# A decoder kernel: the norm's inverse deviation made by GpSimd instead of ScalarE in two of its attention stages

## The reference

```python
def _layernorm(x, axis=-1, eps=1e-05):
    m = jnp.mean(x, axis=axis, keepdims=True)
    v = jnp.var(x, axis=axis, keepdims=True)
    return (x - m) / jnp.sqrt(v + eps)
...
    x = _layernorm(x + _L0_attn_ref(x, ...), axis=-1)            # causal attention, softplus squared
    x = _layernorm(x + _L0_xattn_ref(x, ctx_1024, mask, ...), axis=-1)   # cross attention
    x = _layernorm(x + _L0_ffn_ref(x, ...), axis=-1)             # experts
    x = _layernorm(x + _L1_attn_ref(x, ...), axis=-1)            # latent attention
    x = _layernorm(x + _L1_xattn_ref(x, ctx_1024, ctx_1024, ...), axis=-1) # cross attention
    x = _layernorm(x + _L1_ffn_ref(x, ...), axis=-1)             # quantised feed-forward
```

## Time and profile before

| | |
|---|---|
| time, three runs | 609.74, 605.5, 611.02 us; median 609.74 us |
| profiled execution | 609.74 us in all; span from first to last instruction 607.9 us |
| mean granted PE clock over the span | 0.881 of full |
| busy: PE, PEld, DVE, ACT, POOL | 79%, 58%, 72%, 54%, 40% |
| ACT's two norm steps (lines 157 and 164), 64 of each | 288 and 199 ns mean, one column of 128 rows |
| instructions: PE, DVE, ACT, POOL | 5411, 900, 729, 274 |

### The profile page before, as it was taken

How to read it: one execution, slowest core, us unless ns; L and a number is a source line. 1 busy time by engine, 2 the same in 40 slices (tenths; PEclk the granted TensorE clock), 3 DMA queues, 4 the chain that set the end, 5 groups by cost and what they waited for, 6 DMA issues and landing times. The chain is left out here.

```text
span 607.9 us, 14410 instructions
## 1 busy us (share of the span) xinstructions
PE 478.4 (79%) x5411; PEld 355.1 (58%) x5418; DVE 438.0 (72%) x900; ACT 329.8 (54%) x729; POOL 245.0 (40%) x274
## 2 busy tenths in 40 slices
PE   3888879999996885999869999989999859600035
PEld 1555557677775753767658888867777654100035
DVE  2589886788886568444556777788889746698976
ACT  1688885566664431333246666655656536925234
POOL 5666664555441124556410000068776400070500
PEclk9789895999999599999969999999999968855558
DMA  6500000000000000000000000000000000000002
GB/s 186 210 3 2 2 6 11 14 16 15 16 8 1 1 1 1 0 1 1 2 10 2 3 3 2 3 15 15 15 16 11 2 2 0 0 0 0 0 0 71
DMA packets 9817, 10.07 MB, mean 17 GB/s; under 512 B 722, under 2 KB 8978, under 8 KB 9748
## 3 DMA queue, kind: packets, MB, share of 16 engines
q1 hardware_dynamic: 9748, 9.15, 4.8%
HBM read 8.10 MB, written 1.05 MB: 15 GB/s over the span
## 5 line engine op out<-in xcount | busy, mean ns | idle before, releaser
L1249 POOL TENSOR_TENSOR e_hid<-e_gated,e_relu 128x512 f32<-128x512 f32 x32 | 40.6, 1269 | 53.8 <-DVE e_gated L1364 53.7
L1226 ACT ACTIVATE e_relu<-bank 128x512 f32<-128x512 f32 x36 | 21.5, 598 | 53.2 <-PE bank L1098 44.1
L1120 PEld LDWEIGHTS bank<-body_sb,e_hid 128*128 128x128 f32 x288 | 37.6, 195 | 21.5 <-issue 12.9
L616 DVE TENSOR_REDUCE rowmax<-bank 128x16 f32<-128x1024 f32 x32 | 39.2, 1224 | 13.9 <-PE bank L520 13.7
L130 POOL TENSOR_TENSOR xb<-X,made_bias 128x128 f32<-128x128 f32 x32 | 14.5, 456 | 81.9 <-DVE r L140 77.3
L1364 DVE TENSOR_TENSOR e_gated<-e_relu,bank 128x512 f32<-128x512 f32 x32 | 22.0, 687 | 33.4 <-PE bank L1108 21.3
L1120 PE MATMUL bank<-body_sb,e_hid 128*128 128x128 f32 x288 | 39.1, 281 | 2.5 <-DVE r L1336 1.8
L1098 PE MATMUL bank<-e_xTc,body_sb 128*128 128x512 f32 x72 | 37.8, 607 | 1.3 <-DVE e_gated L1364 1.0
L170 DVE TENSOR_SCALAR X<-r,meanvar,rstd 128x128 f32<-128x128 f32 x64 | 35.6, 557 | 3.2 <-ACT rstd L164 3.1
L242 POOL TENSOR_TENSOR a_spread_heads<-qk,head_sb 128x512 f32<-128x512 f32 x32 | 32.8, 1045 | 11.8 <-ACT qk L337 11.8
L1431 PE MATMUL bank<-head_sb,q_col 128*1 128x128 f32 x5 | 1.7, 332 | 45.2 <-DVE q_col L1537 45.2
(11 more groups left out here) (271 smaller groups left out, 1482.0 us busy)
## 6 DMA issues: line engine op xcount, KB each, us to landing
body_sb<-in_body SPq DMA_DIRECT2D x3, 946.0 KB, 11.0
kvT<-in_ctxT SPq DMA_DIRECT2D x32, 64.0 KB, 2.0
out<-X SPq DMA_DIRECT2D x4, 256.0 KB, 2.3
body_sb<-in_body SPq DMA_DIRECT2D x1, 945.5 KB, 7.5
X<-in_x SPq DMA_DIRECT2D x1, 896.0 KB, 7.6
head_sb<-in_head SPq DMA_DIRECT2D x1, 536.0 KB, 5.4
mid_sb<-in_mid SPq DMA_DIRECT2D x1, 448.0 KB, 3.6
X<-in_x SPq DMA_DIRECT2D x1, 128.0 KB, 2.1
```

Of the source, the lines that this page charges most:

```text
L616: nc.vector.tensor_reduce(m.rowmax[:, :], psS.rearrange("p i (h k) -> p (i h) k", k=T), AX.X, ALU.max).then_inc(s["max_done"].sem, 1)
L1120: mm = nc.tensor.matmul(psY[:, t * D:(t + 1) * D], m.hid[:, n % DEEP, t * P:(t + 1) * P], w2, start=(j == 0 and t == 0), stop=(j == MM - 1 ...
L1226: nc.scalar.activation(m.relu[:, n % DEEP, :], psZ[n % 2][:, :], ACT.Relu).then_inc(s["relu_ready"], 1)
L1249: nc.gpsimd.tensor_tensor(m.hid[:, n % DEEP, :], a, m.relu[:, n % DEEP, :], ALU.mult).then_inc(s["hid_ready"], 1)
```

## The change

In the causal and the latent stage the two steps of ACT's queue are gone. POOL gets two steps in their place: an addition of eps (`shifted_variance`) and a power of -0.5 (`power`), on one column of 128 rows each, with the exponent as a second tile that is filled once. They use the same semaphores as before. The two cross stages keep ACT's steps. POOL's lead in the first block goes from 2 to 1. The diff, with unchanged wrappers left out:

```diff
+    def shifted_variance(self, pool, t, par):
+
+        wait(pool, self.s["var_ready"], t + 1)
+        wait(pool, self.s["rstd_ready"], t)
+        self.nc.gpsimd.tensor_scalar(self.m.lnvar[:, :], self.m.meanvar[:, 1:2], EPS, None, ALU.add).then_inc(self.s["lnvar_done"].sem, 1)
+
+    def power(self, pool, t, par):
+
+        wait(pool, self.s["lnvar_done"], t + 1)
+        wait(pool, self.s["x_new"], t)
+        self.nc.gpsimd.tensor_tensor(self.m.rstd[:, :], self.m.lnvar[:, :], self.m.minus_half[:, :], ALU.pow).then_inc(self.s["rstd_ready"].sem, 1)
...
 # causal stage, POOL
-            run(mask_queries, 2), run(add_bias, 3), run(square, 3)
+            run(mask_queries, 2), run(shifted_variance, 4), run(power, 4), run(add_bias, 3), run(square, 3)
...
 # causal stage, ACT
-            run(copy_values, 1), run(log_variance, 4), run(copy_turned, 0), run(rstd, 4), run(square, 2)
+            run(copy_values, 1), run(copy_turned, 0), run(square, 2)
...
 # latent stage, POOL
-            run(add_bias, 3)
+            run(add_bias, 3), run(shifted_variance, 3), run(power, 3)
...
 # latent stage, ACT
-            run(copy_queries0, 1), run(log_variance, 4), run(rstd, 4), run(copy_turned, 0), run(copy_cq, 0)
+            run(copy_queries0, 1), run(copy_turned, 0), run(copy_cq, 0)
...
 # first block
-                   cross_attention(nc, m, w2, s2, before), lead=(2, 0, 0, 0), loads=loads)
+                   cross_attention(nc, m, w2, s2, before), lead=(1, 0, 0, 0), loads=loads)
```

More of the change, by code:

```diff
@@ L254, in add_bias, with shifted_variance, power @@
             tail.add_bias(pool, t, par)
+        def shifted_variance(t, par):
+            tail.shifted_variance(pool, t, par)
+        def power(t, par):
+            tail.power(pool, t, par)
         def slot(at, cur):
             run = Turn(at, cur)
-            run(mask_queries, 2), run(add_bias, 3), run(square, 3)
+            run(mask_queries, 2), run(shifted_variance, 4), run(power, 4), run(add_bias, 3), run(square, 3)
         return slot
@@ L830, in copy_outputs @@
                                  ACT.Copy).then_inc(s["oT_ready"].sem, 1)
[L832 to L836, removed]
         def slot(at, cur):
@@ L1732, in decoder @@
         m.eps = sb("eps", [P, 1])
+        m.minus_half = sb("minus_half", [P, 1])
         m.xb = sb("xb", [P, 2, P])
@@ L1794, in _ @@
                 pool.memset(m.eps[:, :], EPS)
+                pool.memset(m.minus_half[:, :], -0.5)
                 pool.memset(m.magic[:, :], MAGIC)
```

## The result

| | before | after |
|---|---|---|
| time, median of the runs in one comparison | 607.62 us (603.58 to 611.02, 4 runs) | 701.42 us (700.85 to 703.19, 4 runs) |
| span of the profiled execution | 607.9 us | 699.1 us |
| mean granted PE clock | 0.881 | 0.826 |

The ratio of the times is 1.155, with a 95% interval from 1.147 to 1.164: the change costs 94 us. The forecast was 696 us, in a range from 668 to 714.

What follows compares the result with a forecast made beforehand. The prediction took DVE, never idle in a causal slot, to bound the kernel. Its terms, 68 + 7 + 3.5 - 0.5 + 8.5 = 86.5 us, on top of 609.7 gave 696 us, range 668 to 714.

Steps and rivals of the forecast that it cites:

- the ring: Causal stage: DVE's variance, POOL's norm and square, PE's outputs, spreading and scores run in a row, once per tile.
- The tile: Causal stage: one tile takes 10.5 us at mostly low clock, against 5.30 before; 68 us over 13 tiles.
- The tail: Causal tile, end of scores to residual: 1.9 us at full clock, 2.7 us at the low clock.
- The clock: Causal stage: PE waits 3.2 us and more per tile, so its granted clock is near half between 30 and 170 us.
- clock stays high: Rival in the causal stage: PE's bursts keep the clock high, 43 us instead of 68, 671 us in all; chance 0.17.
- The dear power: Rival on POOL: power 1.04 and addition 0.46 us instead of 0.4 and 0.2, 711 us in all; chance 0.15.
- Into the first cross stage: From the causal stage's last tiles: 7 us for tiles 14 and 15, and 3.5 us before the cross stage's maximum.
- little caught up: First cross stage: part of the delay of its maximum, 4.3 us instead of 0.5, is regained, leaving 3.5 us.
- The shorter lead: POOL's lead only decides whether one rope_sum stands before or after steps that wait longer anyway; costed at nothing.
- The latent stage: Inside it, without ACT's two steps, the turned tile's copy comes earlier: a gain of 0.5 us, at most 1.
- The handover: End of the latent stage into the second cross stage: two rope sums stand behind norms on POOL, costing 8.5 us.
- The faster case: Rival in the causal stage: apply moves away from POOL's multiplication and gets cheaper, winning 10 us, 599 us; chance 0.02.

Runs made afterwards that it cites:

- e1_causal_only: The changed kernel with the latent stage put back as before, so only the causal stage is changed: 688.05 us, ratio 1.130.
- e8_gap_both: The changed kernel with POOL's norm one slot later in both stages, in the causal one between xb and square: 612.13 us, ratio 1.008.
- e7_gap: The changed kernel with only the causal norm one slot later on POOL, between xb and square: 628.38 us, ratio 1.031.

## Why the prediction was right

- **What bounds the kernel, and the ring.** Shown: DVE had no idle time in a causal slot, and now waits at the denominators (68.6 us) and the clamp (12.3 us), each for the engine that the prediction names. The wait at the denominators is 4.57 us in a tile, where the prediction named some 3; its own terms at half clock (2.3 + 0.1 + 1.9) give 4.3. Taking out the square alone left the ring through the spreading; taking the norm out of both took 73 us off.
- **The tile, 10.5 us predicted, 10.24 in the row of waits, 10.21 on average.** To the end of the square 2.3 predicted, 2.38 measured: the addition 0.22 (0.2 taken) and the power 0.57 (0.4 taken, ends 0.1 and 1.04). Outputs to scores 4.9, measured 4.83. Handing over 0.1, measured 0.26. The tail was the term mis-sized: 2.7 us at half clock, 1.86 measured, since the clock was up again by then. Residual to variance 0.9, measured 0.91. For the stage: 68 us predicted, 63.8 measured.
- **The clock.** Predicted near half from 30 to 170 us, with a late rise in some bursts; it rose in every one: 0.66 to 0.67 in each window. The rival "clock stays high" asked for 8.6 us a tile and 671 us. The filler matmuls made that case by hand: 8.48 us, and 676 us with four tiles in which the clock had fallen. The page "TensorE: Matmul & The Clock Gate" of the Trainium skill (Part 1), by which a burst starts low after an idle stretch, agrees with this trace: 1.90 us for outputs behind a wait of 3.63, 0.71 for the projection at the burst's end.
- **The dear power** (711 us) does not hold: 0.57 us, and 8 us or rather less for the whole kernel when it is replaced.
- **Into the first cross stage: 7 and 3.5 us predicted, 7.2 and 7.0 measured.** The 3.5 was too small. From the last variance's end to the maximum, 4.3 us were predicted and 5.5 measured (183.96 to 189.45), since the scores behind the wait ran at half clock (8 matmuls of line 532 took 1.95 us there, 1.03 in the dense part). The "little caught up" was the wrong way: 2.1 us more were lost on the cross stage's next tile.
- **The shorter lead "costs nothing"** was wrong as an argument, though the sum doesn't feel it. With the norm in the gap, lead 1 cost 2.7 us between residuals 13 and 15 and lead 2 about 5 us after residual 15. For the changed order itself lead 2 was not tried: by the order of the queues the norm of tile 15 would stand on POOL ahead of the spreading of keys that DVE's first maximum needs, and the variance of tile 15 stands on DVE behind that maximum, a circle that could not end. So the lead is part of the change, and not a free choice.
- **The latent stage: -0.5 us predicted, +0.3 measured inside.** The gain on ACT's side did not show. The +1.0 us in the stretch that ends with its first residual is not the latent stage's: that stretch took the same 208.84 us in e1_causal_only, with the latent stage as before, and 207.33 in e8_gap_both. The handover: 8.5 predicted, 12.5 measured. The first rope sum was late by 4.2 us (4.3 predicted); what was missed is again the half clock behind the wait (scores of 8 matmuls in 1.99 us where the dense stretch has 1.03, twice) and 1.5 us more on the next tile.
- **Sum.** The terms that were too large by 4.2 us (the causal tiles) stand against those too small by 3.5, 4.0, 0.8 and 0.2 us, and the 1.0 us that belongs to none of them: 86.5 predicted, 91.2 measured in the spans. The forecast was near in part because the misses were on both sides, and because it stood on 609.7 us for the kernel before, 2 us above the median beside which the change was timed.
- **The faster case** (599 us): apply did become 0.34 us, and it was worth nothing in this order, as predicted. Its price of 10 us was too high even for the kernel before, where the best arrangement brought 4.

## What to carry to other kernels

When a step is moved to another engine, its duration matters less than its place: look which work stands behind it in the new queue, and follow that work back to whoever makes the moved step's input. If that work is what the maker of the input waits for next, the two engines can no longer overlap, and everything on the path is done in a row; here two instructions of 0.8 us together cost 64 us over 13 tiles, some 23 of it by the lower clock, and nothing in the slots when they stood where POOL idled anyway. Look at the first and last tiles too: each handover between stages has its own order, and a place that is free inside may cost 5 us there.

## What the hardware showed that I had not expected

- A power on one column took 568 ns on GpSimd, where an addition took 221 and a product 190.
- A chain shortened by 0.4 us did not make its tile shorter: with a shorter wait the granted clock rose later in the burst, and the spacing stayed at 10.24 us. Whether it is held at that value by the clock alone I did not test.
- Apply took 0.34 us alone, and 0.34 to 0.35 where it had begun at least 0.12 us ahead of a POOL instruction, which in the case of the square then took 1.07 to 1.13 us instead of 1.04. Where the POOL instruction was under way, or followed within 0.02 us, apply ended 0.07 to 0.10 us behind the end of that instruction: 1.15 us in most causal tiles of the kernel before, 1.05 in e7_gap beside the square, 0.43 to 0.70 where less was left of it (and 0.34 again where 0.06 to 0.24 us were left). Yet making it short in the kernel before gave 0 to 0.7%. The rest of those 0.8 us turned into waits of DVE.
- Matmuls that nobody needs made the kernel with the waits 25 us faster.
